# Graph attention over a sparse neighbour matrix: neighbour bits peeled in fewer dependent steps, the cap and the ELU folded into neighbouring operations

## The chip, the cores and the metric

The kernel runs on one core of one Trainium2 chip. The metric is the device time of one execution in microseconds, as the median of three runs.

## The reference

For 8192 nodes with 128 features each (`x`, float32) and an 8192 x 8192 int32 matrix `adj` of zeros and ones (a one with probability 0.000244, so two neighbours to a row on average), one layer of graph attention, added to `x` and normalised:

```python
h = x @ W                                   # W: 128 x 128
e = (h @ a1)[:, None] + (h @ a2)[None, :]   # a1, a2: the halves of a
e = jnp.where(e > 0, e, 0.2 * e)
e = jnp.where(adj > 0, e, -9e15)
attention = softmax(e, axis=1)
y = x + elu(attention @ h)
return (y - mean(y)) / sqrt(var(y) + 1e-5)  # over the 128 features
```

`adj` is 256 MiB; everything else is small.

## The kernel before

Rows are worked on in tiles of 128, two tiles make a pair (`PAIR = 2`), two pairs a loop body (`GROUPS = 2`); there are 32 pairs. Nothing dense is computed from `adj`. Each pair passes through a software pipeline of six stages, and in one step (i, g) each engine works on several pairs at once: `now`, and p1 to p5, the pairs one to five before it. The order in each engine's queue is written by hand: `step` in each engine's block, a loop over bodies, and then the last pair, `final`, written out with back1 to back5, the pairs one to five before it. That last part has no new load beside it, and is called the drain here.

The stages of a pair:
- SyncE loads `adj` in half rows (128 rows x 4096 columns, 2 MiB each) into four slots.
- ScalarE squares each half and sums it, for the number of ones in a row (L577). TensorE folds each half's 4096 columns to 512 (L682, L686): eight blocks of 512 columns are added with weights 2^b, plus a small term that carries the column number. VectorE takes the eight largest of the 512 (`pick`, L904).
- `lists` (L910 to L941) turns these 4 x 8 numbers a row into neighbour codes: the mask of eight bits is split into its leading bit and the rest (two peels), each becomes a candidate, and the 16 largest remain, of which ten are used (`SLOTS`). `found` counts the real ones, `cap` holds a very large number for a real slot and -9e15 for an empty one.
- TensorE adds up `found` over the rows (`count_starts`), VectorE makes `ends`, `below_end` and `row_edge` (`route`, L947 to L954), a matrix that sends each row's slots to a list of 640 edges; TensorE applies it (`fill_edges`, L701), VectorE reads out the indices (`indices`), GpSimd gathers the neighbours' rows of `x` with five indirect transfers (L503).
- GpSimd makes `edge_row` (L364), VectorE the neighbours' scores (`neighbour_scores`, t_slot at L989), TensorE sends them back to their rows (`send_scores`, L711), VectorE makes the scores (`scores`, L997 to L1003), ScalarE their exponents (L582), VectorE the shares (`weights`, `edge_weights`), GpSimd `spread` (L382; in the last two pairs VectorE, L376), TensorE sums the neighbours (`sum_neighbours`) and multiplies by W (`times_W`).
- ScalarE takes the exponent of h (L588). `finish` on VectorE (L1026 to L1039) makes ELU as max(h + 1, min(exp h, 1)) - 1, adds x and takes mean and variance. GpSimd makes the norm's factors (`norm_factors`, L466 to L469), ScalarE scales (L600); for the last two pairs VectorE scales itself (`scale_late`, L1051).
- SyncE stores only after the last gather.

On VectorE a helper orders dependent operations: `v.after(instruction)` lets the instruction count up a semaphore and makes the engine wait for it. An instruction that isn't in `v.after` is followed by the next without a wait.

VectorE's queue in the loop is finish(p4), route(p1), neighbour_scores(p2), pick 0, indices(p1), pick 1, scores and weights(p2), picks 2 and 3, lists(now), edge_weights(p2). GpSimd's is norm_factors(p4), mark_empty, tally and gather(p1), spread_weights(p2), edges_to_rows(p1). In the drain, for the step of `final`, VectorE runs pick 0, route(back1), finish(back4), neighbour_scores(back2), indices(back1) and the rest, and GpSimd edges_to_rows(back1) ahead of spread_weights(back2). TensorE has products in the drain that only keep its clock up (`keep_warm`, L783).

Of the kernel before, what the change touches and what calls it, by code (L numbers as in the profile page):

```python
# [55 lines left out]
def graph_attention(nc, x, adj, W, a, out):  # L56
    fp32, i32, u32, bf16 = mybir.dt.float32, mybir.dt.int32, mybir.dt.uint32, mybir.dt.bfloat16
    ACT, ALU, AX = mybir.ActivationFunctionType, mybir.AluOpType, mybir.AxisListType

    N, D = x.shape  # L60
    P = 128
# [4 lines left out]
    FOLD = HALF // BITS  # L66
    assert FOLD == 512
    PAIR = 2
    GROUPS = 2
    BODY = PAIR * GROUPS  # L70
# [4 lines left out]
    UNIT = 2.0 ** -23  # L75
    PEELS = 2
    EXP_BITS = 0x7f800000
    FIRST_EXP = 127 + 9
    COL_0 = FOLD * (FIRST_EXP + BITS - 1) + HALF
    NO_CODE = COL_0 - N - FOLD  # L80
    EDGES = CHUNKS * P // PAIR

    def pieces(t):
# [18 lines left out]
    with ExitStack() as stack:  # L102
        sb = lambda name, shape, dt: stack.enter_context(nc.sbuf_tensor(name, shape, dt))
# [4 lines left out]
        x_sb = sb("x_sb", [P, TILES, D], fp32)  # L108
# [8 lines left out]
        col_no = sb("col_no", [P, FOLD], bf16)  # L117
        col_bits = sb("col_bits", [P, 1], i32)
        exp_bits = sb("exp_bits", [P, 1], i32)
        half_base = sb("half_base", [P, 2 * PAIR, 8], i32)  # L120
        row_id = sb("row_id", [P, TILES], i32)
        offset = sb("offset", [P, P], i32)
# [14 lines left out]
        s_all = sb("s_all", [P, TILES], fp32)  # L137
# [8 lines left out]
        top_map = sb("top_map", [P, 2 * PAIR, 8], fp32)  # L146
        top_int = sb("top_int", [P, 2 * PAIR * 8], i32)
        top_col = sb("top_col", [P, 2 * PAIR * 8], i32)
        top_code = sb("top_code", [P, 2 * PAIR * 8], fp32)
        rest_code = sb("rest_code", [P, 2 * PAIR * 8], fp32)  # L150
        from_base = sb("from_base", [P, 2 * PAIR * 8], fp32)
        lead = sb("lead", [P, PEELS, 2 * PAIR * 8], i32)
        cand = sb("cand", [P, PEELS, PAIR, 2 * 8], fp32)
# [34 lines left out]
        spread = sb("spread", [P, PAIR, SPAN, P], fp32)  # L188
        x_att = sb("x_att", [P, PAIR, P], fp32)
        empty_diag = sb("empty_diag", [P, GROUPS, PAIR, P], fp32)  # L190
        z_one = sb("z_one", [P, PAIR, D], fp32)
        z_exp = sb("z_exp", [P, GROUPS, PAIR, D], fp32)
        elu = sb("elu", [P, PAIR, D], fp32)
        stats = sb("stats", [P, PAIR, 6], fp32)
        mean_var = sb("mean_var", [P, GROUPS, PAIR, 2], fp32)
        var_eps = sb("var_eps", [P, PAIR], fp32)
# [189 lines left out]
        with nc.Block() as block:  # L386
# [173 lines left out]
            def _(act):  # L560
# [23 lines left out]
                def exp_elu(j, g):  # L584
                    act.wait_ge(h_made, count(j, g))
                    if not first(j):
                        act.wait_ge(h_read, count(j, g) - GROUPS)
                    nc.scalar.activation(z_exp[:, g, :, :], h_of(j, g)[:, :, 0:D], ACT.Exp).then_inc(elu_exp, 1)  # L588

                def copy_sums(j, g):  # L590
# [264 lines left out]
            def _(dve):  # L855
# [4 lines left out]
                nc.vector.memset(minus_one[:], -1.0)  # L860
                nc.vector.memset(eps_all[:], EPS)
                nc.vector.memset(exp_bits[:], EXP_BITS)
                nc.vector.memset(col_bits[:], FOLD - 1)
                for t in range(PAIR):
                    nc.vector.memset(tile_edge[:, t:t + 1], float(t * EDGES))
# [40 lines left out]
                def lists(j, g):  # L906

                    flat = [P, 2 * PAIR * 8]
                    dve.wait_ge(picked, j * HALVES + (g + 1) * 2 * PAIR)
                    v.after(nc.vector.tensor_scalar(top_int[:], top_map[:].rearrange("p q s -> p (q s)"),  # L910
                                                    1.0 / UNIT, float(FOLD // 2), ALU.mult, ALU.add))
                    v.after(nc.vector.tensor_tensor(top_col[:], top_int[:], col_bits[:, 0:1].to_broadcast(flat),
                                                    ALU.bitwise_and))
                    nc.vector.tensor_tensor(from_base[:], half_base[:].rearrange("p q s -> p (q s)"), top_col[:],
                                            ALU.subtract)
                    v.after(nc.vector.tensor_tensor(top_code[:], top_int[:], top_col[:], ALU.subtract))
                    v.after(nc.vector.tensor_tensor(lead[:, 0, :], top_code[:].bitcast(i32),
                                                    exp_bits[:, 0:1].to_broadcast(flat), ALU.bitwise_and))
                    v.after(nc.vector.tensor_tensor(rest_code[:], top_code[:], lead[:, 0, :].bitcast(fp32),
                                                    ALU.subtract))  # L920
                    v.after(nc.vector.tensor_tensor(lead[:, 1, :], rest_code[:].bitcast(i32),
                                                    exp_bits[:, 0:1].to_broadcast(flat), ALU.bitwise_and))
                    v.after(nc.vector.scalar_tensor_tensor(
                        cand[:].rearrange("p k t s -> p k (t s)"), lead[:], FOLD * 2.0 ** -23,
                        from_base[:].unsqueeze(1).to_broadcast([P, PEELS, 2 * PAIR * 8]), ALU.mult, ALU.add))

                    for t in range(PAIR):
                        last = nc.vector.max(sent[:, t, 0:8], cand[:, :, t, :])
                    v.after(last)
                    for t in range(PAIR):  # L930
                        last = nc.vector.match_replace(cand_rest[:, :, t, :], sent[:, t, 0:8], cand[:, :, t, :], 0.0)
                    v.after(last)
                    for t in range(PAIR):
                        last = nc.vector.max(sent[:, t, 8:16], cand_rest[:, :, t, :])
                    v.after(last)
                    if not (first(j) and g == 0):
                        dve.wait_ge(diag_made, count(j, g) - 1)
                        dve.wait_ge(tallied, count(j, g) - 1)
                    v.after(nc.vector.tensor_scalar(is_code[:], sent[:, :, 0:SLOTS], float(NO_CODE), None, ALU.is_gt))
                    nc.vector.reduce_sum(found, is_code[:], AX.X).then_inc(listed, 1)  # L940
                    nc.vector.tensor_scalar(cap[:, g, :, :], is_code[:], 1e30, NEG, ALU.mult, ALU.add)  # L941
# [51 lines left out]
                def scores(j, g):  # L993
                    slots = [P, PAIR, SLOTS]
                    dve.wait_ge(t_sent, count(j, g))
                    mine = s_all[:, bass.ds(j * BODY + g * PAIR, PAIR)]
                    v.after(nc.vector.tensor_tensor(score[:], t_row_ps, mine.unsqueeze(2).to_broadcast(slots),  # L997
                                                    ALU.add))
                    v.after(nc.vector.scalar_tensor_tensor(score_l[:], score[:], ALPHA, score[:],
                                                           ALU.mult, ALU.max))  # L1000
                    v.after(nc.vector.tensor_tensor(score_l[:], score_l[:], cap[:, g, :, :], ALU.min))
                    v.after(nc.vector.reduce_max(row_max[:], score_l[:], AX.X))
                    nc.vector.tensor_tensor(score_e[:], score_l[:],  # L1003
                                            row_max[:].unsqueeze(2).to_broadcast(slots),
                                            ALU.subtract).then_inc(scored, 1)
# [16 lines left out]
                def finish(j, g):  # L1022

                    mine = bass.ds(j * BODY + g * PAIR, PAIR)
                    dve.wait_ge(elu_exp, count(j, g))
                    v.after(nc.vector.tensor_scalar(z_one[:], z_exp[:, g, :, :], 1.0, None, ALU.min))  # L1026
                    nc.vector.scalar_tensor_tensor(elu[:], h_of(j, g)[:, :, 0:D], 1.0, z_one[:], ALU.add, ALU.max
                                                   ).then_inc(h_read, 1)
                    dve.wait_ge(h_read, count(j, g))
                    if not first(j):  # L1030
                        dve.wait_ge(norm_ready, count(j, g) - GROUPS)
                    v.after(nc.vector.scalar_tensor_tensor(x_sb[:, mine, :], elu[:], -1.0, x_sb[:, mine, :],
                                                           ALU.add, ALU.add))
                    for t in range(PAIR):
                        tile = j * BODY + g * PAIR + t
                        last = nc.vector.bn_stats(stats[:, t, :], x_sb[:, bass.ds(tile, 1), :])
                    v.after(last)
                    for t in range(PAIR):
                        last = nc.vector.bn_aggr(mean_var[:, g, t, :], stats[:, t, :])  # L1039
                    if not is_late(j, g):  # L1040
                        last.then_inc(stats_ready, 1)
                        return
                    v.after(last)
                    nc.vector.tensor_scalar(late_var[:, g, :], mean_var[:, g, :, 1], EPS, None, ALU.add
                                            ).then_inc(late_ready, 1)
# [189 lines left out]
```

## Time and profile before

| | |
|---|---|
| median of 3 runs | 715.1 us (714.99 to 716.7) |
| the profiled execution | 715.11 us |
| its span, first to last instruction | 713.3 us |
| TensorE matmul busy | 555.4 us (78%) |
| ScalarE busy | 521.0 us (73%) |
| VectorE busy | 480.9 us (67%), 2054 instructions |
| GpSimd busy | 444.8 us (62%) |
| read from HBM | 283.18 MB, 403 GB/s over the span |

Times in the profile are from the start of the span. PE is TensorE, PEld its weight loads, ACT ScalarE, DVE VectorE, POOL GpSimd, SP SyncE. The slices cut the span into 40 equal parts and give each engine's busy share in tenths.

### The profile page before, as it was taken

To read this page: it belongs to the slowest core of one execution; us is meant where nothing else is said; L and a number is where in the kernel's file an instruction comes from. 1 tells how busy PE (TensorE), PEld (TensorE's weight loads), DVE (VectorE), ACT (ScalarE), POOL (GpSimd) and SP (SyncE) were. 2 spreads that over 40 slices of the span, in tenths; PEclk is the share of its full clock that TensorE was granted. 3 is DMA by queue.
4 is the path that set the end of the run, shared out by engine and by line. 5 is a ranking of instruction groups with operands and counts; after the bars stand their busy time and mean duration, and the time that the engine had idled before them with its cause. 6 is when DMAs were issued, how large, how long until landed. Compare 5 with 4: busy or idle time off the path is not lost.

```text
span 713.3 us, 11958 instructions
## 1 busy us (share of the span) xinstructions
PE 555.4 (78%) x3082; PEld 346.3 (49%) x3082; DVE 480.9 (67%) x2054; ACT 521.0 (73%) x414; POOL 444.8 (62%) x675
## 2 busy tenths in 40 slices
PE   0858978787789877877988877777888888777884
PEld 0323455453456554543655545445555555444564
DVE  2473777786766677767586676686666777774885
ACT  0847778787878787878787778787887888787711
POOL 2015468766656776676476666776667667766862
PEclk9987999997988899997898999999998889999988
DMA  9999999999999999999999999999999999999417
GB/s 352 328 417 426 425 426 424 426 426 425 426 427 427 425 430 428 426 427 427 426 426 425 428 429 426 429 427 427 427 425 429 427 427 427 427 427 423 163 40 213
DMA packets 34582, 285.57 MB, mean 400 GB/s; under 512 B 5512, under 2 KB 13856, under 8 KB 18048
## 3 DMA queue, kind: packets, MB, share of 16 engines
q1 hardware_dynamic: 29008, 276.83, 92.9%
q0 software_dynamic: 5120, 8.42, 3.3%
q8 instruction: 9, 0.15, 0.1%
q10 hardware_dynamic: 432, 0.07, 0.1%
q14 instruction: 13, 0.11, 0.0%
HBM read 283.18 MB, written 4.19 MB: 403 GB/s over the span
## 4 chain that ended last, share of the span: by engine, by line
DMA 71%; ACT 10%; PE 9%; issue 5%; DVE 3%; SPq 1%; ACTq 0%; POOLq 0%; POOL 0%; DVEq 0%
DMA adj_sb<-in_adj 69%; ACT adj_squared L577 10%; PE fold L686 5%; DMA a_sb<-in_L_gnn_a 2%; PE x_att_ps L739 1%; PE misc L711 1%; PE fold L682 1%; SPq L402 1%; PE fold L783 1%; PE small L701 1%; DVE below_end L950 0%; PE small L720 0%; PE x_att_ps L742 0%; DVE spread L376 0%; DVE x_sb L1051 0%
## 5 line engine op out<-in xcount | busy, mean ns | idle before, releaser
L577 ACT ACTIVATE adj_squared<-adj_sb 128x4096 bf16<-128x4096 int32 x128 | 462.6, 3614 | 114.8 <-DMA adj_sb<-in_adj 114.1
L686 PE MATMUL fold<-adj_sb,bit_ident 128*128 128x512 bf16 x1024 | 303.9, 447 | 0.2 <-DMA adj_sb<-in_adj 0.2
L503 POOL DMA_INDIRECT nb<-in_x,index x160 | 165.2, 1032 | 93.5 <-issue 63.4
L686 PEld LDWEIGHTS fold<-adj_sb,bit_ident 128*128 128x128 bf16 x1024 | 109.4, 107 | 150.6 <-issue 61.6
L682 PE MATMUL fold<-col_no,ident_bf 128*128 128x512 bf16 x128 | 53.0, 414 | 117.8 <-DMA adj_sb<-in_adj 117.6
L904 DVE MAX8 top_map<-fold 128x8 f32<-128x512 f32 x128 | 89.5, 699 | 69.9 <-PE fold L686 67.6
L364 POOL TENSOR_SCALAR edge_row<-row_iota,edge_in 128x128 f32<-128x128 int32 x186 | 128.6, 705 | 0.1
L382 POOL TENSOR_TENSOR spread<-edge_row,edge_w 128x384 f32<-128x384 f32 x60 | 54.2, 922 | 76.0 <-DVE edge_w L1020 76.0
L682 PEld LDWEIGHTS fold<-col_no,ident_bf 128*128 128x128 bf16 x128 | 15.9, 124 | 135.8 <-issue 89.3
L483 POOL TENSOR_SCALAR empty_diag<-ident,counts 128x128 f32<-128x128 f32 x64 | 39.4, 621 | 59.4 <-DVE counts L940 34.5
L739 PEld LDWEIGHTS x_att_ps<-spread,nb 128*128 128x128 f32 x372 | 57.4, 221 | 7.4 <-issue 3.8
L739 PE MATMUL x_att_ps<-spread,nb 128*128 128x128 f32 x372 | 59.3, 302 | 0.0
L711 PE MATMUL misc<-t_slot,edge_row 128*128 128x10 f32 x384 | 48.9, 261 | 0.1
L965 DVE COPY edge_in<-small 128x90 f32<-128x90 f32 x32 | 8.0, 249 | 58.6 <-PE small L701 58.4
L711 PEld LDWEIGHTS misc<-t_slot,edge_row 128*128 128x128 f32 x384 | 47.0, 197 | 0.5
L701 PE MATMUL small<-sent,row_edge 128*128 128x18 f32 (+1 forms) x384 | 41.7, 246 | 3.5 <-DVE row_edge L954 3.5
L701 PEld LDWEIGHTS small<-sent,row_edge 128*128 128x128 f32 (+1 forms) x384 | 40.0, 172 | 6.9 <-DVE row_edge L954 4.8
L720 PEld LDWEIGHTS small<-share,row_edge 128*128 128x128 f32 (+1 forms) x384 | 40.1, 172 | 2.2 <-DVE share L1011 0.3
L720 PE MATMUL small<-share,row_edge 128*128 128x10 f32 (+1 forms) x384 | 40.9, 239 | 0.1
L985 DVE CUSTOM_DVE_ANT_0 dot<-nb,wa_bc 128x128 f32<-128x128 f32 x160 | 39.5, 302 | 0.0
L954 DVE SCALAR_TENSOR_TENSOR row_edge<-edge_no,sent,below_end 128x320 f32<-128x320 f32 x64 | 35.5, 596 | 1.1
L582 ACT ACTIVATE weight<-score_e 128x20 f32<-128x20 f32 x32 | 7.0, 218 | 30.9 <-DVE score_e L1003 30.9
(122 smaller groups left out, 630.8 us busy)
## 6 DMA issues: line engine op xcount, KB each, us to landing
adj_sb<-in_adj SPq DMA_DIRECT2D x127, 2048.0 KB, 16.2
out<-x_sb SPq DMA_DIRECT2D x2, 1536.0 KB, 10.7
nb<-in_x,index POOLq DMA_INDIRECT x160, 2.6
adj_sb<-in_adj SPq DMA_DIRECT2D x2, 1024.0 KB, 15.1
out<-x_sb SPq DMA_DIRECT2D x5, 128.0 KB, 2.5
out<-x_sb SPq DMA_DIRECT2D x1, 384.0 KB, 10.0
W_sb<-in_L_gnn_W ACTq DMA_DIRECT2D x1, 64.0 KB, 7.8
x_sb<-in_x SPq DMA_DIRECT2D x4, 0.5 KB, 17.7
```

The lines of the kernel that those rows point to most:

```text
L364: last_one = eng.tensor_scalar(edge_row[:, g, t, k, :], row_iota[:, t * P:(t + 1) * P], edge_in[:, c, ROW_COL:ROW_COL + 1], None, ALU.is_e ...
L382: last_one = eng.tensor_tensor(spread[:, t, :, :], edge_row[:, g, t, :, :], mine.unsqueeze(2).to_broadcast([P, SPAN, P]), ALU.mult)
L503: nc.gpsimd.indirect_dma_start(out=nb_of(j, g)[:, c, :], out_offset=None, in_=x[:, :], in_offset=bass.IndirectOffsetOnAxis(ap=index[:, g, ...
L577: nc.scalar.activation(adj_squared[:, h % 2, :], adj_sb[:, h % LOAD_SLOTS, :], ACT.Square, accum_out=half_sum[:, h:h + 1]).then_inc(square ...
L682: nc.tensor.matmul(fold[:, h % LOAD_SLOTS, :], ident_bf[:], col_no[:], start=True, stop=False)
L686: last = nc.tensor.matmul(fold[:, h % LOAD_SLOTS, :], bit_ident[:, b, :], adj_low[:, h % LOAD_SLOTS, b * FOLD:(b + 1) * FOLD, 0], start=Fa ...
L701: last = nc.tensor.matmul(edge_in_ps[lo:hi, c, :], row_edge[:, g, t, e:e + hi - lo], sent[:, t, :], start=True, stop=True)
L711: last = nc.tensor.matmul(t_row_ps[:, t, :], edge_row[:, g, t, k, :], t_slot[:, c, :], start=k == 0, stop=k == SPAN - 1)
L720: last = nc.tensor.matmul(share_ps[lo:hi, c, :], row_edge[:, g, t, e:e + hi - lo], share[:, t, :], start=True, stop=True)
L739: nc.tensor.matmul(x_att_of(j, g)[:, t, 0:P], nb_of(j, g)[:, c, :], spread[:, t, k, :], start=k == 0, stop=False)
L904: nc.vector.max(top_map[:, q, :], fold[:, h % LOAD_SLOTS, :]).then_inc(picked, 1)
L985: last = nc.vector.tensor_tensor_reduce(out=dot[:, c, :], in0=nb_of(j, g)[:, c, :], in1=wa_bc[:, 0, :], scale=1.0, scalar=0.0, op0=ALU.mul ...
```

## The change

Three edits on VectorE, and one wait on ScalarE that goes with the third.

In `lists` the code is no longer made from the integer by subtraction ahead of the first peel. A float 2^8 times as large is made straight from the maxima, beside the integer; its exponent bits are the first peel's leading bit, and both peels' exponents are masked at once, by a mask that keeps four of the exponent's bits, so that an empty mask gives a code below all real ones. In `scores` the cap is applied as the row's own score is added, one operation a tile, ahead of the leaky ReLU. In `finish`, ELU plus x is made as (max(h, 0) + x) + min(exp h, 1), with the constant -1 left out: it shifts a whole row by the same amount, and the norm takes it out. The buffer of the exponent is now read later, so ScalarE waits for the statistics of two pairs before.

```diff
-    FIRST_EXP = 127 + 9
+    LIFT = 2.0 ** 8
+    KEPT_BITS = 0b00010111 << 23
+    FIRST_EXP = 16
     COL_0 = FOLD * (FIRST_EXP + BITS - 1) + HALF
-    NO_CODE = COL_0 - N - FOLD
+    NO_CODE = COL_0 - N
...
+        kept_bits = sb("kept_bits", [P, 1], i32)
...
-        top_code = sb("top_code", [P, 2 * PAIR * 8], fp32)
-        rest_code = sb("rest_code", [P, 2 * PAIR * 8], fp32)
+        peel = sb("peel", [P, PEELS, 2 * PAIR * 8], fp32)
+        top_lead = sb("top_lead", [P, 2 * PAIR * 8], i32)
...
                 def exp_elu(j, g):
                     act.wait_ge(h_made, count(j, g))
                     if not first(j):
-                        act.wait_ge(h_read, count(j, g) - GROUPS)
+                        act.wait_ge(stats_ready, count(j, g) - GROUPS)
...
+                nc.vector.memset(kept_bits[:], KEPT_BITS)
...
                     dve.wait_ge(picked, j * HALVES + (g + 1) * 2 * PAIR)
-                    v.after(nc.vector.tensor_scalar(top_int[:], top_map[:].rearrange("p q s -> p (q s)"),
-                                                    1.0 / UNIT, float(FOLD // 2), ALU.mult, ALU.add))
+                    maps = top_map[:].rearrange("p q s -> p (q s)")
+                    nc.vector.tensor_scalar(peel[:, 0, :], maps, LIFT / UNIT, LIFT * (FOLD // 2), ALU.mult, ALU.add)
+                    v.after(nc.vector.tensor_scalar(top_int[:], maps, 1.0 / UNIT, float(FOLD // 2), ALU.mult, ALU.add))
+                    nc.vector.tensor_tensor(top_lead[:], peel[:, 0, :].bitcast(i32),
+                                            exp_bits[:, 0:1].to_broadcast(flat), ALU.bitwise_and)
                     v.after(nc.vector.tensor_tensor(top_col[:], top_int[:], col_bits[:, 0:1].to_broadcast(flat),
                                                     ALU.bitwise_and))
-                    nc.vector.tensor_tensor(from_base[:], half_base[:].rearrange("p q s -> p (q s)"), top_col[:],
-                                            ALU.subtract)
-                    v.after(nc.vector.tensor_tensor(top_code[:], top_int[:], top_col[:], ALU.subtract))
-                    v.after(nc.vector.tensor_tensor(lead[:, 0, :], top_code[:].bitcast(i32),
-                                                    exp_bits[:, 0:1].to_broadcast(flat), ALU.bitwise_and))
-                    v.after(nc.vector.tensor_tensor(rest_code[:], top_code[:], lead[:, 0, :].bitcast(fp32),
+                    nc.vector.tensor_tensor(peel[:, 1, :], peel[:, 0, :], top_lead[:].bitcast(fp32), ALU.subtract)
+                    v.after(nc.vector.tensor_tensor(from_base[:], half_base[:].rearrange("p q s -> p (q s)"), top_col[:],
                                                     ALU.subtract))
-                    v.after(nc.vector.tensor_tensor(lead[:, 1, :], rest_code[:].bitcast(i32),
-                                                    exp_bits[:, 0:1].to_broadcast(flat), ALU.bitwise_and))
+                    v.after(nc.vector.tensor_tensor(
+                        lead[:].rearrange("p k s -> p (k s)"), peel[:].rearrange("p k s -> p (k s)").bitcast(i32),
+                        kept_bits[:, 0:1].to_broadcast([P, PEELS * 2 * PAIR * 8]), ALU.bitwise_and))
...
                     dve.wait_ge(t_sent, count(j, g))
-                    mine = s_all[:, bass.ds(j * BODY + g * PAIR, PAIR)]
-                    v.after(nc.vector.tensor_tensor(score[:], t_row_ps, mine.unsqueeze(2).to_broadcast(slots),
-                                                    ALU.add))
+                    for t in range(PAIR):
+                        last = nc.vector.scalar_tensor_tensor(
+                            score[:, t, :], t_row_ps[:, t, :], s_all[:, bass.ds(j * BODY + g * PAIR + t, 1)],
+                            cap[:, g, t, :], ALU.add, ALU.min)
+                    v.after(last)
                     v.after(nc.vector.scalar_tensor_tensor(score_l[:], score[:], ALPHA, score[:],
                                                            ALU.mult, ALU.max))
-                    v.after(nc.vector.tensor_tensor(score_l[:], score_l[:], cap[:, g, :, :], ALU.min))
...
                     dve.wait_ge(elu_exp, count(j, g))
-                    v.after(nc.vector.tensor_scalar(z_one[:], z_exp[:, g, :, :], 1.0, None, ALU.min))
-                    nc.vector.scalar_tensor_tensor(elu[:], h_of(j, g)[:, :, 0:D], 1.0, z_one[:], ALU.add, ALU.max
-                                                   ).then_inc(h_read, 1)
+                    nc.vector.scalar_tensor_tensor(x_plus[:], h_of(j, g)[:, :, 0:D], 0.0, x_sb[:, mine, :],
+                                                   ALU.max, ALU.add).then_inc(h_read, 1)
                     dve.wait_ge(h_read, count(j, g))
                     if not first(j):
                         dve.wait_ge(norm_ready, count(j, g) - GROUPS)
-                    v.after(nc.vector.scalar_tensor_tensor(x_sb[:, mine, :], elu[:], -1.0, x_sb[:, mine, :],
-                                                           ALU.add, ALU.add))
+                    v.after(nc.vector.scalar_tensor_tensor(x_sb[:, mine, :], z_exp[:, g, :, :], 1.0, x_plus[:],
+                                                           ALU.min, ALU.add))
```

## Rows read from the trace of the kernel before

**Rows 1.** The page's slices of the span.
```profile
DMA  9999999999999999999999999999999999999417
```
**Rows 2.** Busy time by stretch (us), with clock, DMA share, GB/s.
```profile
500.00:600.00 100.00, 83.45 (x468) 53.67 (x466) 67.54 (x296) 79.91 (x66) 67.17 (x102) 0.87 1.01 427
...
671.00:713.30 42.30, 28.36 (x179) 21.64 (x177) 29.44 (x131) 9.01 (x17) 21.89 (x37) 0.84 0.40 111
```
**Rows 3.** The chain that ended last, 677 us on: start, us, what.
```profile
677.56 2.84 DVE below_end L950 x2
...
680.42 1.03 DVE row_edge L954 x2
...
695.56 1.25 PE misc L711 x12
...
696.84 0.19 DVE score L997
...
697.05 0.19 DVE score_l L999
...
702.18 0.21 DVE z_one L1026
...
705.85 0.21 DVE z_one L1026
...
708.89 0.60 DVE x_sb L1051 x2
```
**Rows 4.** Timelines of DVE and POOL in the steady part: start, us.
```profile
618.96 0.80 DVE L950 TENSOR_SCALAR below_end<-edge_no,counts 128x320 f32<-128x320 f32 x2
...
617.94 4.29 POOL L364 TENSOR_SCALAR edge_row<-row_iota,edge_in 128x128 f32<-128x128 int32 x6
```
**Rows 5.** Timeline of POOL in the drain.
```profile
664.88 0.31 POOL L466 TENSOR_TENSOR var_eps<-mean_var,eps_all 128x2 f32<-128x2 f32 x1 [1.69 <-DVE mean_var L1039]
...
674.80 3.52 POOL L364 TENSOR_SCALAR edge_row<-row_iota,edge_in 128x128 f32<-128x128 int32 x6
678.29 1.61 POOL L382 TENSOR_TENSOR spread<-edge_row,edge_w 128x384 f32<-128x384 f32 x2
```
**Rows 6.** Line L950 by itself, 677 to 681 us: ns min/median/max.
```profile
L950 DVE TENSOR_SCALAR below_end<-edge_no,counts x2: 372/1452/2531, 677.6 to 680.0; 128x320 f32<-128x320 f32 x2
```
**Rows 7.** Timeline of DVE, the lists of the last pair.
```profile
672.72 0.18 DVE L910 TENSOR_SCALAR top_int<-top_map 128x32 int32<-128x32 f32 x1
...
673.16 0.19 DVE L914 TENSOR_TENSOR from_base<-half_base,top_col 128x32 f32<-128x32 int32 x1
673.27 0.18 DVE L916 TENSOR_TENSOR top_code<-top_int,top_col 128x32 f32<-128x32 int32 x1
...
674.25 0.32 DVE L923 SCALAR_TENSOR_TENSOR cand<-lead,from_base 128x64 f32<-128x64 int32 x1
...
675.69 0.35 DVE L939 TENSOR_SCALAR is_code<-sent 128x20 f32<-128x20 f32 x1
```
**Rows 8.** Timeline of DVE, the finish of back4.
```profile
662.53 0.28 DVE L1026 TENSOR_SCALAR z_one<-z_exp 128x256 f32<-128x256 f32 x1
662.85 0.42 DVE L1027 SCALAR_TENSOR_TENSOR elu<-h_ps,z_one 128x256 f32<-128x256 f32 x1
```
**Rows 9.** Busy time by stretch in the drain; the third last number is the clock.
```profile
678.60:681.49 2.89, 0.00 (x1) 0.00 (x1) 2.85 (x5) 0.00 (x0) 1.53 (x3) 1.00 0.00 0
...
682.80:689.60 6.80, 6.40 (x29) 6.05 (x28) 4.75 (x23) 0.59 (x2) 3.70 (x4) 0.50 0.09 24
689.60:706.00 16.40, 14.37 (x102) 10.89 (x102) 11.20 (x57) 3.77 (x11) 8.88 (x20) 1.00 0.79 219
```
**Rows 10.** Timelines of DVE and ACT in the drain.
```profile
694.38 0.21 DVE L989 TENSOR_TENSOR t_slot<-at_slot,t_edge 128x50 f32<-128x50 f32 x1
...
704.91 0.38 ACT L588 ACTIVATE z_exp<-fold 128x256 f32<-128x256 f32 x1 [0.80 <-PE fold L751]
```
**Rows 11.** Busy time by stretch, when the stores drain.
```profile
708.00:709.00 1.00, 0.00 (x0) 0.00 (x0) 0.11 (x1) 0.00 (x0) 0.69 (x1) 0.50 0.17 44
```

More of the change, by code:

```diff
@@ L190, in graph_attention @@
         empty_diag = sb("empty_diag", [P, GROUPS, PAIR, P], fp32)
-        z_one = sb("z_one", [P, PAIR, D], fp32)
+        x_plus = sb("x_plus", [P, PAIR, D], fp32)
         z_exp = sb("z_exp", [P, GROUPS, PAIR, D], fp32)
-        elu = sb("elu", [P, PAIR, D], fp32)
         stats = sb("stats", [P, PAIR, 6], fp32)
```

## Prediction

> **What bounds the kernel now.** I read the page's slices first: the DMA row stands at 9 in 37 of the 40 slices and falls only in the last three [rows 1]. Then the busy time by stretch: between 500 and 600 us the DMA share is 1.01 while VectorE is busy 67.54 us of 100; after 671 us the share falls to 0.40 and VectorE is busy 29.44 of 42.30 us [rows 2]. The reader should see two regimes. Up to 671 us adjacency arrives as fast as the DMA engines carry it, and VectorE time there buys nothing. The last 42 us drain the pipeline, and only there can the change move the end. So I read next the chain of work that ended last, from 677 us on [rows 3]. It goes from VectorE's below_end (677.56) to row_edge, then through TensorE to 696.81, then through the final tiles' scores and the two last finishes on VectorE.
>
> **What sets the early part of the drain.** below_end of the final tiles, two instructions, takes 2.84 us [rows 3]. The same pair in the steady part takes 0.80 us, beside the same GpSimd work [rows 4]. In the drain GpSimd runs edge_row from 674.80 to 678.32 and spread from 678.29 to 679.90 without a break [rows 5], and the stretched pair ends only at 680.39 [rows 3]. The pair's two instructions last 2,531 and 372 ns [rows 6], so the second begins at about 680.0, just after GpSimd's spread is over. I read the end of the pair as "GpSimd idle, plus some 0.5 us" and not as "lists done, plus 0.8". A saving ahead of below_end is therefore swallowed, unless GpSimd's run itself moves.
>
> **Lists (the peeling).** There are 8 instructions up to and with cand before, and 8 after. Before, the part ahead of cand has six dependent steps and one that follows without a wait: 672.72 to 674.25, 1.53 us. A dependent step costs (1.53 - 0.11) / 6 = 0.24 us here, and one without a wait 0.11 us (673.16 to 673.27) [rows 7]. After, it has four dependent steps and three without a wait: 4 x 0.24 + 3 x 0.11 = 1.29 us, and lead's 64 elements in place of 32 may add a little: cand, with 64 and two operations, lasts 0.32 us against top_int's 0.18, so between 0 and 0.14, and I take 0.03, since the part above the instruction's fixed time is small. That saves 0.2 us. Bounds: 0 if a step without a wait costs as much as one with it, and 2 x 0.24 = 0.48 if the extra independent ones were free. For the end I take 0, since GpSimd covers it: is_code would start at 675.49 in place of 675.69 and was itself held (0.35 us) by edge_row [rows 7, 5]. Without that cover it would be worth the 0.2 us.
>
> **Finish of the pair of tiles four before the last.** In finish the minimum z_one disappears: it costs 662.53 to 662.85, 0.32 us from start to start [rows 8]. The two operations left have the old two's shapes: one reads PSUM and SBUF, one reads two SBUF tensors, 128x256 each. The trace has neither with its new operands: I take no difference, and as the bound one step without a wait more, 0.11 us a finish. The finish that starts at 662.53 is the only thing that lets GpSimd go on: its norm factors idle 1.69 us for mean_var until 664.88, and from there its queue runs on over the gathers to the edge rows at 674.80 and the spread [rows 5]. So GpSimd's block ends 0.32 us earlier, and with it below_end, row_edge and TensorE's start at 681.49. Saved: 0.32 us; bounds 0 and 0.32. The finish's own start hangs, over the row_edge ahead of it and the first fold of its step, on the DMA stream, so it stays.
>
> **TensorE between 681.5 and 695.6.** TensorE is idle from 678.60 to 681.49, its granted clock then falls from 1.00 to 0.50 (1.2 of 2.4 GHz) for 682.8 to 689.6, and is 1.00 after [rows 9]. Gap and work shift together, so I take the shift of 0.32 to pass through whole. The final t_slot is ready at 694.59 [rows 10], while TensorE comes to the product that reads it at 695.56 [rows 3], behind its warming products: VectorE has 0.97 us to spare there, so what scores and finishes save between 681 and 694 counts for nothing.
>
> **Final scores.** Before, three dependent steps lead to row_max; score to score_l is 0.21 us [rows 3]. After, two per-tile operations (the second 0.11 us behind the first) and one dependent step: 0.21 - 0.11 = 0.10 us saved. Bounds: 0 and 0.21. The cap is ready long before. Over this step one rule can be held: the section "The DRAIN you can't avoid" of the page "VectorE: DVE Perf Modes" in the Trainium skill says that chaining without semaphores skips nothing, and that only the number of operations counts; by that rule lists and scores, with their counts unchanged, save nothing, and the total below is 0.96 us. The 0.11 against 0.24 us [rows 7] speaks against it for operations this small.
>
> **The last two finishes.** From 702.18 on the chain is VectorE's: finish, scale, finish, scale. Each z_one costs its start to elu's start, 0.32 us [rows 3, 8], so 2 x 0.32 = 0.64 us. The final pair's exponent must be there by then; its finish moves up by only 0.32 us against the rest, and ScalarE had it ready at 705.29 [rows 10], against z_one in the chain at 705.85 [rows 3]. Bounds: 0.42 (0.11 us more in each) and 0.64.
>
> **Stores.** The DMA engines are still full with output until shortly after 708 us (share 0.17 in the stretch from 708) [rows 11], while the last store waits for the scale that ends at 709.49 [rows 3]. It has over one us of room, so about 1 us can be saved ahead of it. The extra constant is one more memset of one element in the setup, under the adjacency stream that sets the time to 671 us: nothing, and without that cover no more than one step. ScalarE's exponent now waits for the statistics two pairs back in place of the reading of h; those are done a step earlier, so nothing either.
>
> **Sum.** 0 (lists) + 0.32 (GpSimd's block) + 0.10 (scores) + 0.64 (finishes) = 1.06 us. The profiled execution took 715.11 us, span 713.3 and 1.8 around it, which is the median of the three runs (715.1). 715.1 - 1.06 = 714.0 us.
>
> **Rivals.**
> *The long stall goes.* Nothing in the rows says why below_end is stretched in the drain and not in the steady part, beside the same edge_row work [rows 4]. If the altered arrival lets it through, it starts at 677.24 and takes 0.80: row_edge starts 2.35 us earlier than at 680.42. TensorE's idle gap is 0.8 us in place of 2.89, and its clock may then stay up. That gains up to 2.35 + 0.97 = 3.3 us, where t_slot becomes the limit. With the 0.74 of scores and finishes: 711.1 us; at the old clock, 2.35 + 0.74 = 3.1, 712.0 us. For it: the steady rows. Against: the offset of below_end to GpSimd's instructions stays the same if both shift by 0.32, and is_code is caught by the same block. In the Trainium skill, "SBUF — State Buffer", section "Who interferes with whom", has a two-port Vector instruction and a GpSimd one exclude each other for one whole instruction; by that rule the wait would last for one GpSimd instruction of 0.6 to 0.8 us and the time would be near this rival's, and the 2.84 us [rows 3] do not agree.
>
> *The half clock lasts longer.* It lasted 6.8 us [rows 9]. If a shift by 0.3 us makes it last half as long again, 3.4 us more of TensorE's work take twice as long: +1.7 us, 715.7 us, slower than before. For it: one of the three runs before stands at 716.7. Against: TensorE's work after 681.49 has no long gap, before as after. It decides once more than 1.06 us are lost. To be slower by over 0.3% it must double, 717.4 us.
>
> *The half clock is shorter or absent.* TensorE gains up to 3.4 us, but t_slot gives back all but 0.97: 714.0 - 0.97 = 713.1 us.
>
> *GpSimd's block doesn't move, or only the last finishes count.* 715.1 - 0.74 = 714.4, and with an exponent that comes late 714.7 us.
>
> **How the numbers follow.** Forecast (714.0, between 713.7 and 714.4) 0.58; GpSimd's block unmoved 0.12; stall goes 0.17; shorter half clock 0.05; longer half clock 0.08. A difference under 0.3% (2.1 us, outside 713.0 to 717.2) can't be told from no change. Faster: 0.17 and half of the shorter half clock, 0.19. Slower: the worst of the longer half clock, 0.03. Same: 0.78. The range 712.6 to 715.8 leaves out the stall's end and the worst of the clock, 0.20.
>
> **What would show it.** Right: VectorE has 2,023 instructions, z_one gone; the time from top_int to cand is 1.3 us with the new first operation counted; GpSimd's norm factors start at 664.6 and its spread ends at 679.6; below_end still takes over 2 us and ends with it; from the last scores on each finish is 0.32 us shorter; the DMA share stays 1.0 until 671. Wrong: below_end under 1 us (then 711 to 712), a half-clock stretch of another length, or an adjacency stream that ends at another time than 670.8, in which case the steady part was not bound as I say.

## The result, and the profile after

The changed kernel takes 723.97 us (median of four executions, 723.35 to 727.34), against 715.69 us for the kernel before beside it. The ratio is 1.0113, with a 95% interval of 1.009 to 1.0135: slower by 1.1%, where 714.0 us and no telling difference were forecast.

The page of the changed kernel, first its slices and the count of VectorE's instructions, as [rows 1] for before:

```profile
span 721.6 us, 11902 instructions
...
PE 545.4 (76%) x3033; PEld 343.3 (48%) x3082; DVE 473.7 (66%) x2023; ACT 520.9 (72%) x414; POOL 442.0 (61%) x675
...
DMA  9999999999999999999999999999999999999417
GB/s 352 327 421 418 420 416 423 424 417 417 419 420 420 426 420 421 420 421 420 419 422 420 426 419 421 421 417 420 422 425 419 421 421 421 419 421 418 185 27 224
```

VectorE has the 2,023 instructions of the forecast and is less busy than before. The DMA row is the same to the digit, which shows how little a share of busy time says: the engines are as full as before and carry less. Their rate by stretch, in the same columns as [rows 2]:

```profile
500.00:600.00 100.00, 77.07 (x455) 49.88 (x461) 67.36 (x290) 78.82 (x61) 67.23 (x104) 0.91 1.01 421
```

It is 421 GB/s where [rows 2] has 427, with the DMA share at 1.01 in both. The last maximum of the last pair (`pick`), which waits for the stream's last piece, ends at 672.69 us before (0.03 us ahead of top_int in [rows 7]) and at 681.82 here:

```profile
681.12 0.70 DVE L909 MAX8 top_map<-fold 128x8 f32<-128x512 f32 x1 [0.42 <-PE fold L690]
681.85 0.39 DVE L916 TENSOR_SCALAR peel<-top_map 128x32 f32<-128x32 f32 x1
...
683.40 0.23 DVE L928 SCALAR_TENSOR_TENSOR cand<-lead,from_base 128x64 f32<-128x64 int32 x1
...
684.76 0.67 DVE L944 TENSOR_SCALAR is_code<-sent 128x20 f32<-128x20 f32 x1
```

So the stream ends 9.1 us later and the drain behind it is 0.8 us shorter (the spans differ by 8.3). The chain that ended last, in the drain, against [rows 3]:

```profile
686.62 2.59 DVE below_end L955 x2
689.24 1.03 DVE row_edge L959 x2
...
704.39 1.25 PE misc L715 x12
705.67 0.38 DVE score L1002 x2
706.07 0.32 DVE score_l L1006
706.41 0.18 DVE row_max L1008
...
711.12 0.34 DVE x_plus L1032
...
714.38 0.43 DVE x_plus L1032
...
717.18 0.60 DVE x_sb L1056 x2
```

From the last pick to the end of below_end it takes 7.39 us (7.70 before), from there to the final product of TensorE 15.18 (15.17 before), from the start of the scores to x_plus 5.45 (to z_one 5.34 before), and from there to the end of the last scaling 6.66 (7.31 before). That is -0.31, +0.01, +0.11 and -0.65, together -0.84 us.

**Where the stream lost its 9 us.** The trace has a record of every single DMA packet, which the page only sums up. Adjacency goes in packets of 16 KB. Between 100 and 660 us they last 614.7 ns on the mean in the kernel before, apart from 77 of over 650 ns. In the changed kernel 2,143 of them last over 650 ns, 675.3 on the mean, and the rest 614.6. The longer ones come in bunches of 80 once a step of 20 us, in the same 6 us in which the packets of the five gathers into nb travel. The records don't name the engine of a packet; 80 is what 16 engines with one longer packet for each of the five gathers make. Read so, each gather costs each engine some 60.7 ns: 160 gathers make 9.7 us, less the last few, which travel behind the stream; it ends 9.1 us later.

Nothing in the diff touches a gather. What it moves is their destination. The change declares kept_bits, 4 bytes in a place of 32, and peel and top_lead (256 + 128 bytes) for top_code and rest_code (128 + 128), all ahead of nb. So nb starts 160 bytes later in every partition: at byte 173,216 in place of 173,056, the latter a multiple of 512.

### The profile page after: what moved, and what is told of

The parts are those of the page before. It is cut to its first block, busy times and chain, and to the rows that moved or that the text cites. A ratio compares the mean times of both kernels' runs of the same rounds, so it can differ in the third digit from the quotient of the medians.

```text
span 721.6 us, 11902 instructions
## 1 busy us (share of the span) xinstructions
PE 545.4 (76%) x3033; PEld 343.3 (48%) x3082; DVE 473.7 (66%) x2023; ACT 520.9 (72%) x414; POOL 442.0 (61%) x675
## 4 chain that ended last, share of the span: by engine, by line
DMA 74%; PE 11%; ACT 7%; issue 4%; DVE 2%; SPq 1%; ACTq 0%; POOLq 0%; POOL 0%; DVEq 0%
DMA adj_sb<-in_adj 71%; ACT adj_squared L581 7%; PE fold L690 7%; DMA a_sb<-in_L_gnn_a 2%; PE fold L686 1%; SPq L406 1%; PE misc L715 1%; PE fold L787 1%; PE x_att_ps L743 1%; DVE below_end L955 0%; PE small L705 0%; PE small L724 0%; PE x_att_ps L746 0%; PE h_ps L755 0%; DVE spread L380 0%
## 5 line engine op out<-in xcount | busy, mean ns | idle before, releaser
L690 PE MATMUL fold<-adj_sb,bit_ident 128*128 128x512 bf16 x993 | 297.9, 444 | 8.4 <-DMA adj_sb<-in_adj 4.1
L686 PE MATMUL fold<-col_no,ident_bf 128*128 128x512 bf16 x112 | 49.0, 438 | 133.2 <-DMA adj_sb<-in_adj 120.0
L368 POOL TENSOR_SCALAR edge_row<-row_iota,edge_in 128x128 f32<-128x128 int32 x186 | 124.2, 681 | 0.1
L743 PEld LDWEIGHTS x_att_ps<-spread,nb 128*128 128x128 f32 x372 | 53.7, 208 | 7.0 <-issue 3.3
L743 PE MATMUL x_att_ps<-spread,nb 128*128 128x128 f32 x372 | 55.8, 289 | 0.0
L705 PE MATMUL small<-sent,row_edge 128*128 128x18 f32 (+1 forms) x384 | 43.3, 251 | 2.3 <-DVE row_edge L959 2.3
L705 PEld LDWEIGHTS small<-sent,row_edge 128*128 128x128 f32 (+1 forms) x384 | 42.1, 179 | 5.7 <-DVE row_edge L959 2.8
L604 ACT ACTIVATE x_sb<-x_sb,shift,rstd (+1 forms) x60 | 26.0, 482 | 2.6 <-POOL shift L473 2.6
```

The source lines that it names most:

```text
L368: last_one = eng.tensor_scalar(edge_row[:, g, t, k, :], row_iota[:, t * P:(t + 1) * P], edge_in[:, c, ROW_COL:ROW_COL + 1], None, ALU.is_e ...
L686: nc.tensor.matmul(fold[:, h % LOAD_SLOTS, :], ident_bf[:], col_no[:], start=True, stop=False)
L690: last = nc.tensor.matmul(fold[:, h % LOAD_SLOTS, :], bit_ident[:, b, :], adj_low[:, h % LOAD_SLOTS, b * FOLD:(b + 1) * FOLD, 0], start=Fa ...
L705: last = nc.tensor.matmul(edge_in_ps[lo:hi, c, :], row_edge[:, g, t, e:e + hi - lo], sent[:, t, :], start=True, stop=True)
L743: nc.tensor.matmul(x_att_of(j, g)[:, t, 0:P], nb_of(j, g)[:, c, :], spread[:, t, k, :], start=k == 0, stop=False)
```

## The experiments

**nb moved back; nb moved alone; two of the edits alone.** An unused tensor ahead of nb is the whole edit of the first two:

```diff
+        nb_pad = sb("nb_pad", [P, 88], fp32)     # after_nb_aligned, on the changed kernel: 352 bytes
+        nb_pad = sb("nb_pad", [P, 40], fp32)     # before_nb_160, on the kernel before: 160 bytes
         nb = sb("nb", [P, GROUPS + 1, CHUNKS, D], fp32)
```

finish_alone has the change's finish and exp_elu in the kernel before, scores_alone its scores.

> The changed kernel, with one unused tensor of 352 bytes per partition declared ahead of nb, so that nb, the gathers' destination, starts at byte 173,568 (a multiple of 512, as the 173,056 of before) and not at 173,216 (160 past one). The index tensor and everything declared before nb stay where the change put them. Theory 1, the gathers' destination address slows the adjacency packets that are under way beside a gather (80 packets of 16 KB a step last about 671 ns instead of 614, which is 57 ns x 5 a step x 32 steps = 9 us, the whole of the 9.1 us by which the adjacency stream ends later): 714 to 715 us, the stream at 426 to 427 GB/s and ending at about 670.8. Theory 2, it is the altered timing of VectorE that slows the stream: stays at 723 to 724, the stream at 421 GB/s. Theory 3, the address of another tensor than nb (index, edge_row): stays at 723 to 724.

> The kernel of before, no instruction altered, with one unused tensor of 160 bytes per partition ahead of nb, so that nb starts at 173,216, where the change puts it; all that is declared before nb stays. Theory 1 (nb's address): 723 to 725 us, adjacency at 420 to 421 GB/s, packets of about 671 ns beside the gathers. Theory 2 (VectorE's timing): 715 to 716. Theory 3 (another tensor declared before nb): 715 to 716.

> The kernel of before with only the edit to finish and the exponent's wait; nb keeps its address, since the edit's tensors are declared behind it. By the prediction: 0.64 us for the last two finishes and 0.32 for GpSimd's block, 0.96 less than before, about 714.3 to 714.8 us; the pair four before the last starts GpSimd's norm factors 0.32 us earlier. By theory 2 (altered timing slows the stream), if the finish is what does it: 720 us or more. Rival within the drain: GpSimd's block does not move, 0.6 us less.

> The kernel of before with only the edit to scores; no tensor moves. By the prediction 0.10 us less than before, which cannot be told from none. By theory 2, if scores is what slows the stream: 720 us or more. A rival for the step itself: the new operations read two tensors and a scalar and last longer than the 0.16 to 0.18 us of the old, so that the step from the first of them to row_max is not shorter at all.

Measured, with the ratio to the kernel before on the same chip (716.51 us there) and its interval:

| kernel | us | ratio |
|---|---|---|
| after_nb_aligned | 715.62 | 0.9992 (0.9975 to 1.0008) |
| before_nb_160 | 723.97 | 1.0109 (1.0092 to 1.0126) |
| finish_alone | 715.03 | 0.9977 (0.9962 to 0.9992) |
| scores_alone | 715.65 | 0.9985 (0.9972 to 0.9999) |

The two stretches, of after_nb_aligned and then of before_nb_160:

```profile
500.00:600.00 100.00, 80.40 (x464) 51.14 (x463) 68.41 (x299) 79.95 (x66) 67.56 (x105) 0.88 1.01 427
```

```profile
500.00:600.00 100.00, 77.24 (x465) 49.52 (x462) 68.55 (x297) 78.79 (x63) 68.21 (x104) 0.91 1.01 421
```

The 160 bytes alone give the whole loss, and taking them back takes the whole loss back, with every instruction of the change in place. The unused tensor moves nb and all that is declared behind it; of these only nb is written by a DMA in the loop, and the longer packets stand beside the gathers into it, so I take nb as the one that matters. VectorE's altered timing (theory 2) is out, since before_nb_160 has the old timing and the loss; so are tensors declared ahead of nb (theory 3), which stay moved in after_nb_aligned. scores_alone lies 0.15% under before, with an interval that just misses 1, but its drain (37.14 us from the last pick to VectorE's last instruction, against 37.09) has no gain in it, so none is read from it. Its profiled execution took 718.87 us, and not because of the stream: by the packet records the last packet of adjacency landed at 670.1 us, against 670.3 before. TensorE's granted clock was 0.50 there, where it is 1.00 before; it folded the last halves late, and the last pick ended 3.8 us later (676.45 against 672.69). Busy time by stretch, first of before, then of scores_alone:

```profile
664.00:667.00 3.00, 3.00 (x29) 3.00 (x28) 2.79 (x21) 1.45 (x4) 1.84 (x5) 1.00 0.63 265
```

```profile
664.00:667.00 3.00, 3.00 (x15) 2.60 (x14) 1.31 (x12) 0.51 (x2) 1.58 (x4) 0.50 0.62 259
```

So a single profiled execution can lie 3 us off the median of its kernel, as here (718.87 against 715.65).

**Which addresses cost time.** The kernel before with nb_pad of 32, 64, 128 and 256 bytes.

> The kernel of before, nb moved by 32 bytes (173,088: 32 past a multiple of 512; an odd multiple of 32, like the 160 of the change). If what matters is whether the gathered 512-byte rows start on a multiple of 64: slow, 723 to 725 us. If only starts on a multiple of 512 are fast: slow too. If 160 itself is special: 715 to 716.5.

> The kernel of before, nb moved by 64 bytes. If a multiple of 64 is enough: 715 to 716.5 us and no adjacency packets of 671 ns beside the gathers. If a row must lie inside an aligned 512-byte or 256-byte block: slow, 723 to 725. A cost in between would say that it is the number of pieces into which a row falls.

> The kernel of before, nb moved by 128 bytes. By the multiple of 64: 715 to 716.5 us. By the multiple of 256 or 512: 723 to 725.

> The kernel of before, nb moved by 256 bytes. By the multiple of 64 or of 256: 715 to 716.5 us. By the multiple of 512 alone: 723 to 725.

| nb past a multiple of 256 | us | ratio | GB/s, 500 to 600 us |
|---|---|---|---|
| 32 | 726.39 | 1.0156 (1.0138 to 1.0173) | 422 |
| 64 | 725.21 | 1.0140 (1.0123 to 1.0157) | 421 |
| 128 | 724.94 | 1.0133 (1.0116 to 1.0151) | 421 |
| 0 (moved by 256) | 716.46 | 1.0013 (1.0002 to 1.0024) | 427 |

The kernel before took 715.9 us beside them. The rule of a multiple of 64 fails: 64 and 128 are slow, as 32 and 160 are. A multiple of 256 is enough, and the cost is one step, not a slope. In the Trainium skill the section "How a descriptor splits into AXI transactions" of the page "DMA: Bandwidth & Descriptors" says that the first transaction of a descriptor which does not start on a multiple of 256 bytes starts at the 256-byte boundary below; it speaks of reading. A row of 512 bytes would then take three transactions in place of two, an estimate from that page's rule. The runs show the same multiple for the destination of 512-byte rows; that the extra transaction is the mechanism is not shown here.

**Whether the adjacency itself pays.** x_sb and adj_sb start 128 bytes past a multiple of 256 in both kernels. before_all_256 puts them and nb on multiples:

```diff
+        x_pad = sb("x_pad", [P, 32], fp32)
         x_sb = sb("x_sb", [P, TILES, D], fp32)
...
+        nb_pad = sb("nb_pad", [P, 32], fp32)
         nb = sb("nb", [P, GROUPS + 1, CHUNKS, D], fp32)
```

> The kernel of before with unused tensors so that x_sb and adj_sb (both 128 past a multiple of 256 until now) and nb all start on a multiple of 256. It asks whether the adjacency's own destination, 16 KB packets, is subject to what slows the gathers' 512-byte rows. If each 16 KB packet pays for one broken piece at its ends: 14,190 packets in 500 us at 614 ns would become shorter by a few ns each, some 0.5 to 1% of the stream, 709 to 713 us and over 427 GB/s. If only the short rows pay, or the stream is bound elsewhere: 715 to 716.5 us, 427 GB/s.

Measured: 708.33 us, ratio 0.9880 (0.9858 to 0.9903). (The 14,190 packets of the expectation are about those of 560 us and not of 500: 14,123 start between 100 and 660 us in before.) The windows of the load of x, first of before, then of before_all_256:

```profile
20.00:30.00 10.00, 9.05 (x36) 4.30 (x37) 2.71 (x7) 8.93 (x6) 0.00 (x0) 1.00 1.02 334
30.00:40.00 10.00, 8.29 (x23) 3.43 (x21) 8.16 (x25) 5.75 (x4) 2.09 (x3) 1.00 1.06 328
```

```profile
20.00:30.00 10.00, 9.12 (x34) 4.22 (x35) 2.33 (x6) 9.00 (x6) 0.00 (x0) 1.00 1.00 387
30.00:40.00 10.00, 8.61 (x25) 3.72 (x25) 8.16 (x25) 5.93 (x5) 2.09 (x3) 1.00 1.06 426
...
500.00:600.00 100.00, 81.77 (x467) 52.75 (x474) 71.62 (x313) 80.57 (x66) 69.50 (x105) 0.90 1.01 430
```

x comes in rows of 512 bytes too, four to a packet; the packets' median falls from 116 to 89 ns. In these 20 us 1.5 MB more arrive ((53 + 98 GB/s) x 10 us), worth 3.6 us at 420 GB/s. Behind it 427 becomes 430, 0.7% of 630 us or 4 us. Together that is most of the 8.1 us. By the packet records the last packet of adjacency lands at 663.1 us against 670.3 before, 7.2 us earlier, and 3.4 of them are already there at 50 us. The expectation named the stream alone; about half of the gain is the load of x. The profiled execution was the longest of the six all the same, 711.82 us: TensorE's clock was at 0.50 until 663.0 us in it, and the last pick ended only 3.3 us earlier than before.

**The stretched below_end.** In aligned_spread_after_route GpSimd's spread of back2 waits for the last row_edge:

```diff
                 edges_to_rows(nc.gpsimd, *back1)
+                hold(pool, routed, count(*final), pool_spare)
                 spread_weights(nc.gpsimd, *back2)
```

> The changed kernel with nb on a multiple of 256 (as in after_nb_aligned), and in the drain GpSimd's spread of the pair back2 waits until row_edge of the last pair is made. It asks whether GpSimd's spread is what stretches below_end. If below_end's 2.5 us are an unbroken run of GpSimd instructions that lets it in only at its end: the run now ends with edge_row, 1.6 us earlier, the pair of below_end ends about 1.6 us earlier, and, since TensorE's idle gap shrinks to about 1.3 us and its clock may stay at 1.0, the time from the last pick to the end falls from 36.5 us to between 33.5 and 35, 712 to 714.5 us. If the stretch has another cause: it stays, the drain stays at 36.5 or grows, since spread is 1.6 us later, 715 to 716.5.

Measured: 712.47 us, ratio 0.9943 (0.9922 to 0.9963), and the time from the last pick to the last VectorE instruction is 34.29 us against 36.55 in after_nb_aligned. Timelines of GpSimd and VectorE in it:

```profile
674.72 3.61 POOL L369 TENSOR_SCALAR edge_row<-row_iota,edge_in 128x128 f32<-128x128 int32 x6
679.94 1.77 POOL L387 TENSOR_TENSOR spread<-edge_row,edge_w 128x384 f32<-128x384 f32 x2 [1.61 <-DVE row_edge L961]
...
677.74 0.78 DVE L957 TENSOR_SCALAR below_end<-edge_no,counts 128x320 f32<-128x320 f32 x2
```

The pair takes 0.78 us, as in the steady part [rows 4]. TensorE's half clock lasts 3.4 us here in place of 6.8 [rows 9]:

```profile
683.80:687.20 3.40, 3.34 (x16) 3.04 (x15) 3.19 (x16) 0.24 (x2) 2.50 (x3) 0.50 0.07 19
687.20:700.00 12.80, 11.69 (x80) 8.58 (x83) 8.26 (x45) 3.36 (x9) 8.89 (x20) 1.00 0.62 172
```

So the stretch comes from spread following at once behind edge_row; after_all_256_route shows the same below (0.80 us for the pair). It is not below_end's own either. In finish_alone the instruction ahead of it, two elements long, was the one under way, and it took the wait, to the end of spread, while the pair behind it lasted 0.68 us:

```profile
677.88 1.95 DVE L947 TENSOR_TENSOR counts<-sent,counts 128x2 f32<-128x2 f32 x1
679.87 0.68 DVE L949 TENSOR_SCALAR below_end<-edge_no,counts 128x320 f32<-128x320 f32 x2
...
678.20 1.61 POOL L381 TENSOR_TENSOR spread<-edge_row,edge_w 128x384 f32<-128x384 f32 x2
```

Why below_end waits from 677.56 when spread starts only at 678.29 [rows 5], and would have been through by then at 0.45 us, is not explained by it.

**All together.** after_all_256 is the changed kernel with x_pad of 128 and nb_pad of 224 bytes; after_all_256_route has the wait as well.

> The changed kernel with x_sb, adj_sb and nb all on multiples of 256. With no address left that differs in kind from before_all_256, what remains between the two is the change's own work: by the drain of after_nb_aligned against before's, about 0.5 us, so 707.5 to 708.3 us beside the 708.3 of before_all_256. If the altered timing of VectorE cost the stream anything: 709 us or more.

> The same, and GpSimd's spread of back2 in the drain waits until row_edge of the last pair is made. If the two effects add: 0.5 + 2.3 us under before_all_256, 705 to 706 us, the best of all here. If the end of the drain is now set by the stores behind the last gather, less: 706.5 to 708.

Measured: 707.13 us, ratio 0.9877 (0.9852 to 0.9903), and 706.81 us, ratio 0.9869 (0.9840 to 0.9897); the kernel before took 716.33 beside them. Both beat both kernels by over 1% in the median. Between the changed instructions (0.9877) and the old ones (0.9880, on another chip), all on multiples of 256, no difference can be told, and the intervals leave room for some 2 us either way. What the change is worth at fixed addresses is seen only in the drain of single executions: 36.55 us in after_nb_aligned against 37.09 before. The two gains did not add. In after_all_256 the drain is 35.0 us, with the stretch still there (2.3 us) but the half clock falling in two shorter pieces, and 35.5 us with the wait, where the half clock is again one piece of 6.8 us. The stores, which the expectation had for this case, are not what holds the end: from the end of the last scaling to the end of the span it takes 3.7 us, against 3.8 before. That the drain's length hangs on where the clock's fall meets TensorE's work is my reading and wasn't tried, and six executions between 704.7 and 711.1 don't separate the two kernels.

## Why the prediction was wrong

**The steady part.** The prediction said that up to 671 us adjacency arrives as fast as the DMA engines carry it, "and VectorE time there buys nothing". For VectorE's time that is right, and finish_alone and scores_alone show it: between 500 and 600 us the stream's rate is 427 GB/s in both. But "as fast as the DMA engines carry it" took the rate as given, and it is not: it is 430 GB/s in before_all_256 and 421 here. The step that failed is the next one, "and only there [in the drain] can the change move the end". It priced instructions, waits and one memset, and gave the declarations no price; the "extra constant" that it put at nothing takes 32 of the 160 bytes by which they moved nb. Those 160 bytes move the end of the stream by +9.1 us here and by +8.8 us in before_nb_160 (its last pick ends at 681.49 us). The forecast had named an adjacency stream that ends at another time than 670.8 as a sign against it, and it was that sign which came; none of the rivals was.

**Lists.** Forecast: 0.2 us on VectorE, 0 on the end. From the last pick's end to cand: 1.58 us after, 1.56 before. Nothing was gained even on VectorE in this place: peel and top_int, side by side, and the wider lead lasted 0.39, 0.32 and 0.42 us, against means of 0.20, 0.18 and 0.23 over the kernel; GpSimd issues its gathers in that stretch. In after_nb_aligned the same stretch takes 1.25 us, 0.3 less than before, and there GpSimd issues gathers too; so the dependent steps can be saved, against the rule in the prediction by which unchanged counts save nothing, and what lengthened the three instructions here is open. The end did not feel it, as forecast.

**GpSimd's block.** Forecast 0.32 us earlier, measured 0.31 in the changed kernel, and the match is luck. The first link held: from the start of finish to the norm factors it takes 2.02 us, against 2.35 before. But then GpSimd stopped for TensorE's x_att_ps, which it did not do before:

```profile
673.22 0.31 POOL L470 TENSOR_TENSOR var_eps<-mean_var,eps_all 128x2 f32<-128x2 f32 x1 [1.47 <-DVE mean_var L1044]
...
675.52 1.20 POOL L487 TENSOR_SCALAR empty_diag<-ident,counts 128x128 f32<-128x128 f32 x2 [0.48 <-PE x_att_ps L746]
```

Norm factors 0.33 us later would have been done by 675.4 us, still ahead of 675.52 (an estimate from these rows), so the 0.31 us is where x_att_ps stood against the last pick, and not the saving in finish. The two kernels with the new finish and nb on a multiple of 256, finish_alone and after_nb_aligned, show nothing of it: from the last pick to the end of below_end it takes 7.78 and 7.71 us in them, against 7.70 before. That is the rival in which GpSimd's block doesn't move. In finish_alone the new finish starts at 662.39 and its mean_var is ready at 664.06, yet GpSimd reaches its norm factors at 665.02, with no wait, since its own edge_row ends only then. In after_nb_aligned GpSimd, later on, waits 2.27 us for TensorE's x_att_ps:

```profile
663.74 0.31 POOL L471 TENSOR_TENSOR var_eps<-mean_var,eps_all 128x2 f32<-128x2 f32 x1 [0.68 <-DVE mean_var L1045]
...
667.83 1.20 POOL L488 TENSOR_SCALAR empty_diag<-ident,counts 128x128 f32<-128x128 f32 x2 [2.27 <-PE x_att_ps L747]
```

So the step that failed here is "the only thing that lets GpSimd go on": VectorE's mean_var, GpSimd's own edge_row or TensorE's x_att_ps can be the last, and 0.32 us on one of them need not come through.

**below_end and TensorE.** In the changed kernel the stretch stayed and ends with spread as forecast, and the 15.17 us behind it passed through unchanged. The rival that the stretch goes did not happen by this change; its price was about right once the wait on GpSimd made it happen: 2.3 us of drain against 2.35 to 3.3. (Its gap of 0.8 us for TensorE should read 2.89 - 2.35 = 0.54 us; 0.52 was measured.)

**Final scores.** Forecast -0.10, measured +0.11. The start of score to row_max is 0.62 us in scores_alone against 0.64 before: the new operations read PSUM, a scalar and cap, and last 0.22 us in the mean where the old one lasted 0.16, which takes up what the missing step gives. In the changed kernel score_l then took 0.32 us in place of 0.19; GpSimd's counting of rows runs beside it, but it does so before and in scores_alone too, where score_l lasts 0.19, so this is open.

**The last two finishes.** Forecast -0.64, measured -0.65. The drain of finish_alone is 36.62 us against 37.09, and its total ratio is 0.9977, with all of its interval under 1: it is the one edit with both a shorter drain and a lower time. The ratio is 1.6 us, and the drain shows only 0.5 of it.

**The sum.** The drain's forecast was -1.06 us and it came to -0.84, of the right sign and size, but 0.31 of that by luck: with nb in place it comes to -0.54 (after_nb_aligned), which is the last two finishes less what the scores cost. Either is under a tenth of what the addresses did.

## What to carry to other kernels

When a kernel is bound by DMA, read a diff's declarations as carefully as its instructions: work out the new start of every tensor that a DMA writes, above all of those written in rows of 512 bytes, and keep it on a multiple of 256. A DMA share of 1.0 is not a rate: compare GB/s, and when it falls with the share unchanged, look at the single packets and at what travels beside the long ones. An edit that seems to win or lose about 1% in such a kernel has to be measured again with the addresses held fixed.

## What the runs showed of the hardware that was not expected

- A gather of 512-byte rows to a destination off a multiple of 256 bytes (32, 64, 128 or 160 past it) lengthens 16 KB packets of another queue that are under way beside it, 16 to a gather, from 614.7 to about 675 ns; on a multiple of 256 it does not. The gathers' own 4 KB packets grew only from 164 to 167 ns. Why the cost lands on the other queue's packet is open.
- The 16 KB packets themselves gain a little (614.7 to 611.8 ns each, 427 to 430 GB/s) and packets of four 512-byte rows a lot (116 to 89 ns) from starting on a multiple of 256.
- A VectorE tensor_scalar of 320 elements lasts 2.5 us when GpSimd's two-input spread follows its edge_row, and 0.45 us when spread is kept back, though it starts before spread does in both. In finish_alone a tensor_tensor of two elements lasts 1.95 us in the same place.
